# Keys and values of a cross attention, made in the prologue or inside the units that use them later

## The reference, cut to what matters

```python
q = xn @ Wq                       # xn: x normalised twice, (2, 512, 128)
kv = context @ Wkv                # (2, 154, 96) @ (96, 2048)
k, v = jnp.split(kv, 2, axis=-1)
dots = jnp.einsum('bhnd,bhmd->bhnm', q, k) * scale
dots = jnp.where(mask, dots, -jnp.inf)
attn = jax.nn.softmax(dots, axis=-1)
out = jnp.einsum('bhnm,bhmd->bhnd', attn, v)
return out.reshape(...) @ Wo + bo
```

## Time and profile before

| | us |
|---|---|
| median of 3 runs (lowest, highest) | 501.18 (499.8, 506.23) |
| span of the profiled execution | 502.9 |
| prologue up to the first scores | 33.0 |
| first scores to the transposes of unit 0 | 22.3 |
| one unit of the first cross attention | 12.4 |
| PE, DVE, ACT, POOL busy, whole span | 418.0, 315.5, 239.3, 72.2 |

### The profile page before, as it was taken

One profiled execution on the slowest core, in us unless ns is written; L12 is line 12 of the kernel. 1 busy time (PEld: TensorE's weight loads), 2 busy tenths in 40 slices (PEclk: granted clock), 3 DMA queues, 4 the chain that ended last, 5 costly groups with the idle time before them and its releaser, 6 DMA issues.

```text
span 502.9 us, 6017 instructions
## 1 busy us (share of the span) xinstructions
PE 418.0 (83%) x1990; PEld 216.3 (43%) x1990; DVE 315.5 (63%) x830; ACT 239.3 (48%) x683; POOL 72.2 (14%) x104
## 2 busy tenths in 40 slices
PE   4978789899897999998575978578899997989576
PEld 2443445466453844676333644313222232324245
DVE  4555977666873337546888683296687768671242
ACT  2325566745663273302534654005577776577220
POOL 5260500001000010002397020300000002000110
PEclk9979999999999997999988898956999999999956
DMA  8900000000000000000000002703800000000000
GB/s 230 220 1 1 1 0 2 1 1 0 3 1 0 1 0 0 1 1 1 1 0 1 1 0 93 159 0 117 136 1 2 2 1 3 1 1 1 23 0 21
DMA packets 15742, 12.93 MB, mean 26 GB/s; under 512 B 2880, under 2 KB 14879, under 8 KB 15519
## 3 DMA queue, kind: packets, MB, share of 16 engines
q1 hardware_dynamic: 15150, 11.64, 9.8%
q10 hardware_dynamic: 561, 0.90, 0.7%
HBM read 8.80 MB, written 3.67 MB: 25 GB/s over the span
## 4 chain that ended last, share of the span: by engine, by line
PE 49%; DVE 27%; ACT 14%; DMA 5%; issue 3%; SPq 1%; ACTq 0%; POOL 0%; DVEq 0%
PE pC L637 6%; PE pT L686 6%; PE pS L536 5%; DVE PT L1067 5%; ACT PT L806 5%; PE pS L380 4%; PE pC L426 4%; PE pT L478 3%; PE pS L629 3%; DVE mx L1243 3%; DVE mx L1042 3%; DVE spare L1067 3%; PE pC L413 2%; PE pT L349 2%; ACT PT L920 2%
## 5 line engine op out<-in xcount | busy, mean ns | idle before, releaser
L1243 DVE TENSOR_REDUCE mx<-pS 128x2 f32<-128x1024 f32 x64 | 77.0, 1221 | 26.9 <-PE pS L629 26.8
L920 ACT ACTIVATE PT<-pT 128x512 f32<-128x512 f32 x128 | 72.8, 597 | 25.7 <-PE pT L686 23.5
L380 PE MATMUL pS<-space,xT 128*128 128x308 f32 x192 | 69.3, 471 | 8.3 <-ACT PT L806 2.9
L806 ACT ACTIVATE PT<-pS,nm 128x154 f32<-128x154 f32 x136 | 51.3, 400 | 47.1 <-DVE nm L1045 47.1
L1343 POOL TENSOR_SCALAR ve<-mv 128x4 f32<-128x4 f32 x10 | 2.3, 229 | 358.1 <-DVE mv L969 358.1
L686 PE MATMUL pT<-space 128*128 128x512 bf16 x128 | 47.7, 387 | 7.0 <-ACT PT L920 3.1
L629 PE MATMUL pS<-space 128*128 128x512 bf16 x128 | 43.3, 425 | 10.8 <-DMA space<-parts_scratch 4.9
L413 PE MATMUL pC<-PT,space 128*128 128x512 f32 (+2 forms) x144 | 49.4, 620 | 2.8 <-DVE PT L1054 1.5
L380 PEld LDWEIGHTS pS<-space,xT 128*128 128x128 f32 x192 | 35.2, 210 | 30.6 <-issue 16.6
L1042 DVE TENSOR_REDUCE mx<-pS 128x4 f32<-128x616 f32 x48 | 38.3, 797 | 11.5 <-PE pS L384 7.5
L1067 DVE TENSOR_SCALAR PT<-PT,rz 128x154 f32<-128x154 f32 x136 | 37.7, 341 | 1.2
(11 more groups left out here) (209 smaller groups left out, 662.1 us busy)
## 6 DMA issues: line engine op xcount, KB each, us to landing
space<-parts_scratch SPq DMA_DIRECT2D x8, 384.0 KB, 7.2
parts_scratch<-space SPq DMA_DIRECT2D x6, 256.0 KB, 2.4
parts_scratch<-space SPq DMA_DIRECT2D x2, 384.0 KB, 2.5
parts_scratch<-space SPq DMA_DIRECT2D x6, 128.0 KB, 2.3
space<-in_L_xattn_Wq_dram SPq DMA_DIRECT2D x1, 512.0 KB, 3.8
x<-in_x_dram SPq DMA_DIRECT2D x2, 256.0 KB, 6.8
space<-in_L_xattn_Wo_dram SPq DMA_DIRECT2D x1, 512.0 KB, 7.0
space<-in_L_ffn_up_w_dram SPq DMA_DIRECT2D x1, 512.0 KB, 6.0
```

What stands on the lines that cost most here:

```text
L380: last = mm(ps[:, 512 * i:512 * i + 2 * T], xT[:, b, q * P:(q + 1) * P], a.KP[:, b, G4 * g + 2 * i:G4 * g + 2 * i + 2, :].rearrange("p h k ...
L806: last = A.activation(pq(n, u, q)[:, j * T:(j + 1) * T], ps[:, c:c + T], ACT.Exp, bias=nm[:, u % 2, q, j:j + 1], scale=XSCALE, accum_out=z ...
L920: A.activation(PT[:, 4 * kt + j, :], ps[:, :], ACT.Exp, scale=SSCALE)\
L1243: V.tensor_reduce(mx[:, u % 2, k // 2, j:j + 2], ps[:, :].rearrange("p (i k) -> p i k", i=2), AX.X, ALU.max).then_inc(freed(("ss", u, k)), 1)
```

## The change

The prologue makes only the first four transposes of Wq and the keys of group 0 (two key blocks, four heads). Group 1's keys are made in the head of `cross` between scores 1 and 2 of unit 0; the second four transposes and group 2's keys in unit 0, group 3's in unit 1, after `turn(u)` and ahead of scores 2; batch 0's values stay in the head, batch 1's move into units 2 and 3 at the same place. KT holds eight heads instead of sixteen and moves into OT's space; the memsets of its zeros halve. On DVE the statistics of batch 0 stand ahead of the keys' copies, `normalise(0, 0)` and batch 1's statistics behind the mask's conversion, and the four instructions for `allow` move into the head of `cross`, behind group 1's copies. The second layer's calls have new arguments and the same content.

```diff
+        KH = 2 * G4
-            kt = m.take(H * B * T) if n else PT[:, 0:10, :].rearrange("p c s -> p (c s)")[:, 0:H * B * T]
-            a.KT = kt.rearrange("p (h b k) -> p h b k", h=H, b=B)
+            kt = m.take(KH * B * T) if n else OT_[:, 4 * S:4 * S + KH * B * T]
+            a.KT = kt.rearrange("p (h b k) -> p h b k", h=KH, b=B)
...
+            def group_keys(a, g):            # PE
+                keysT(a, (2 * g, 2 * g + 1))
+                for h in range(G4 * g, G4 * g + G4):
+                    keys(a, h)
...
                 scores(a, 0, 1)
                 if n == 0:
-                    context_values(a, 0, (0, 1, 2, 3, 4))
+                    group_keys(a, 1)
                 scores(a, 0, 2)
                 if n == 0:
-                    context_values(a, 1, (0, 1))
+                    context_values(a, 0, (0, 1, 2))
                 scores(a, 0, 3)
                 if n == 0:
-                    context_values(a, 1, (2, 3, 4))
+                    context_values(a, 0, (3, 4))
...
                     turn(u)
+                    if n == 0 and u == 0:
+                        weightsT(a, (4,))
+                        group_keys(a, 2)
+                    if n == 0 and u == 1:
+                        group_keys(a, 3)
+                    if n == 0 and u == 2:
+                        context_values(a, 1, (0, 1, 2))
+                    if n == 0 and u == 3:
+                        context_values(a, 1, (3, 4))
                     scores(a, u + 1, 2)
...
             context()
-            weightsT(xa[0])
-            keysT(xa[0])
-            for h in range(H0):
-                keys(xa[0], h)
+            weightsT(xa[0], (0,))
+            group_keys(xa[0], 0)
             columns()
...
-                exponentials(0, 0, 2)        # ACT, head of cross
+                exponentials(0, 0, 1)
+                if n == 0:
+                    group_keys(a, 1)
+                exponentials(0, 1, 3)
                 if n == 0:
                     act.wait_ge(consts, 1)
-                    context_values(a, 0, (0, 2, 4))
-                exponentials(0, 2, 3)
-                if n == 0:
-                    context_values(a, 1, (0,))
+                    context_values(a, 0, (0, 2))
                 exponentials(0, 3, 4)
                 if n == 0:
-                    context_values(a, 1, (2, 4))
+                    context_values(a, 0, (4,))
...
                     copy_chunk(u, 4)
                     copy_chunk(u, 2)
+                    if n == 0 and u in (0, 1):
+                        group_keys(a, u + 2)
+                    if n == 0 and u == 2:
+                        context_values(a, 1, (0, 2))
+                    if n == 0 and u == 3:
+                        context_values(a, 1, (4,))
...
                     maxima(a, 0, 0, 2)       # DVE, head of cross
-                    dve.wait_ge(consts, 1)
-                    context_values(a, 0, (1, 3))
+                    group_keys(a, 1)
+                    allowed()
                     maxima(a, 0, 2, 3)
                     divide(0, 0)
-                    context_values(a, 1, (1,))
+                    dve.wait_ge(consts, 1)
+                    context_values(a, 0, (1,))
                     maxima(a, 0, 3, 4)
                     divide(0, 1)
-                    context_values(a, 1, (3,))
+                    context_values(a, 0, (3,))
...
                     divide(u + 1, 1)
+                    if n == 0 and u == 0:
+                        weightsT(a, (4,))
+                    if n == 0 and u in (0, 1):
+                        group_keys(a, u + 2)
+                    if n == 0 and u in (2, 3):
+                        context_values(a, 1, (2 * u - 3,))
...
-            V.memset(xa[0].KT[DH:P, 0:H0:2, :, :], 0.0)
-            V.memset(xa[0].KT[0:DH, 1:H0:2, :, :], 0.0).then_inc(kt_pads, 1)
-            weightsT(xa[0])
-            keysT(xa[0])
-            for h in range(1, H0, 2):
-                keys(xa[0], h)
-                if h in (1, 5):
-                    statistics(0, h // 4)
-                if h == 11:
-                    normalise(0, 0)
+            V.memset(xa[0].KT[DH:P, 0:KH:2, :, :], 0.0)
+            V.memset(xa[0].KT[0:DH, 1:KH:2, :, :], 0.0).then_inc(kt_pads, 1)
+            weightsT(xa[0], (0,))
+            statistics(0, 0)
+            group_keys(xa[0], 0)
             dve.wait_ge(W["mask"], 16)
             V.tensor_scalar(maskb[:, :, :], masku[:, :, :], -BLOCKED, BLOCKED, ALU.mult, ALU.add)\
                 .then_inc(mask_ready, 1)
-            seq(V.tensor_copy(maskf[:, :, :], masku[:, :, :]))
-            (three more on allow; all four are now allowed())
+            normalise(0, 0)
+            statistics(0, 1)
             cross(xa[0])
```

More of the change, by code:

```diff
@@ L321, in columns, with weightsT @@
                 tr(ps[:, 0:E], gwr[:, :], ident[0:E, 0:E]).then_inc(full("gateT"), 1)
-            def weightsT(a):
+            def weightsT(a, firsts):
                 n = a.n
                 pe.wait_ge(W[f"Wq{n}"], 16)
-                for c0 in range(0, a.H // 2, 4):
+                for c0 in firsts:
                     ps = claim("T", ("wqT", n, c0))
@@ L336, in keysT @@
                 pe.wait_ge(ctx_pads, n + 1)
-                for c in range(a.H // 2):
+                for c in cs:
                     ps = claim("C", ("kT", n, c))
@@ L454, in cross @@
                 if n == 0:
-                    weightsT(xa[1])
-                    keysT(xa[1])
+                    weightsT(xa[1], (0,))
+                    keysT(xa[1], range(H1 // 2))
                     for h in range(4):
@@ L741, in xt, with keysT @@
                     cp(xT[:, b, :], ps[:, :]).then_inc(freed(("xT", stage, b)), 1)
-            def keysT(a):
-                for c in range(0, a.H // 2, 2):
+            def keysT(a, cs):
+                for c in cs:
                     ps = filled(act, ("kT", a.n, c))
@@ L747, in keysT @@
                         r = slice(DH * i, DH * (i + 1))
-                        last = cp(a.KT[r, 2 * c + i, :, :].rearrange("p b k -> p (b k)"), ps[r, 0:B * T])
+                        last = cp(a.KT[r, (2 * c + i) % KH, :, :].rearrange("p b k -> p (b k)"), ps[r, 0:B * T])
                     last.then_inc(freed(("kT", a.n, c)), 1)
@@ L765, in context_values, with group_keys @@
                     last.then_inc(freed(("v", n, b, k)), 1)
+            def group_keys(a, g):
+                keysT(a, (2 * g,))
+                for h in (G4 * g, G4 * g + 2):
+                    keys(a, h)
             def self_in(b):
@@ L833, in cross @@
                 if n == 0:
-                    keysT(xa[1])
+                    keysT(xa[1], range(0, H1 // 2, 2))
                     for h in (0, 2):
@@ L990, in weightsT, with keysT @@
                         .then_inc(freed(("wqT", a.n, c0)), 1)
-            def keysT(a):
-                for c in range(1, a.H // 2, 2):
+            def keysT(a, cs):
+                for c in cs:
                     ps = filled(dve, ("kT", a.n, c))
@@ L1013, in context_values, with group_keys @@
                     ins.then_inc(freed(("v", a.n, b, k)), 1)
+            def group_keys(a, g):
+                keysT(a, (2 * g + 1,))
+                for h in (G4 * g + 1, G4 * g + 3):
+                    keys(a, h)
             def parts(u):
@@ L1117, in cross @@
                 if n == 0:
-                    weightsT(xa[1])
-                    keysT(xa[1])
+                    weightsT(xa[1], (0,))
+                    keysT(xa[1], range(1, H1 // 2, 2))
                     for h in (1, 3):
```

18 lines of the change are left out of this document (9 added, 9 removed).

## The result

The changed kernel takes 516.66 us (median of four runs, 513.29 to 518.41) against 503.71 us for the kernel before, timed beside it: a ratio of 1.029 with a 95% interval of 1.024 to 1.034. It is slower, and by more than the 8.8 us of the forecast.

What follows compares the result with a forecast made beforehand. PE's own queue was taken as the chain within a unit, nearly full in both places. Units' 18.05 us less 10.4 us gained earlier gave +7.7, 508.9 us by the median; +1.0 for the clock made 510 us, range 504 to 517.

Steps and rivals of the forecast that it cites:

- The start: Prologue: with less work there, the first scores issue at 19.7 us, 13.3 us earlier.
- The head: First scores to unit 0's transposes: these start at 43.9 us, keeping 11.3 of 13.3 us; gain up to scores 2, 10.4 us.
- the sum: Unit costs of 18.05 us less 10.4 us gained earlier: +7.7 us, 508.9 us by the median.
- The units: Units 0 to 3: extra work ahead of scores 2 costs 5.7, 5.7, 3.75 and 2.9 us, together 18.05.
- the clock's term: Head of the attention: PE's new wait may bring the clock down, costing 2.0 us; half taken, +1.0 us.
- The verdict's side: Whole kernel: within 2% (10.0 us) counts as same, chance 0.58; slower 0.38, faster 0.04.
- The range: Whole kernel: 504 to 517 us, leaving out the not-slower case and a little above the 514.5 us rival.
- The page's rule: Trainium skill page: frequent short idles between matmul groups, from cycling through PSUM, let the clock swing; would make 514.5 us likely.
- The rival of falls in the ping-pong of units 0 and 1: Units 0 and 1: clock falls during key making, two of up to 1.8 us, give 514.5 us; chance 0.22.
- The rival on the other side: Units 0 to 3: copies' round trips overlap PE's gaps, units cost 6.15 us, total 496.9 us; chance 0.14.

Runs made afterwards that it cites:

- the spread kernel: Changed kernel with only the place of the extra work inside units 0 to 3 altered, set between scores and values: 503.94 us, ratio 1.007 to the kernel before.
- The second profile of before: Profile of the unchanged kernel before, timed again against itself with no edit: 501.02 us, ratio 0.999.
- all three profiles of the changed kernel: Profiles of three measurements of the same changed kernel, without edits: 516.66, 512.39 and 512.55 us, ratios 1.029, 1.023 and 1.021 to the kernel before.
- the filled one: Changed kernel with unread transposes in four of PE's waits and unit 0's chunk 4 ahead of chunk 3: 509.01 us, ratio 1.012 to the kernel before.
- the mended kernel with the chunk order: Changed kernel with work spread in units, head reordered, normalise(0, 1) after unit 0's work, unit 0's chunk 4 ahead of chunk 3: 500.09 us, ratio 0.998.
- filled: The mended kernel with the chunk order, plus 21 unread transposes in three of PE's waits: 496.74 us, ratio 0.988 to the kernel before.
- the later measurements: The same changed kernel timed a second and a third time, no edit: 512.39 and 512.55 us, ratios 1.023 and 1.021 to the kernel before.
- the kernel with the head mended: Changed kernel with mask row-sum instructions behind maxima 2 and value chunk 0 copied ahead of tile 2's exponentials: 509.24 us, ratio 1.018 to the kernel before.
- the late normalisation: Changed kernel with work spread and head reordered, plus DVE's normalise(0, 1) moved to the end of unit 0's work: 499.89 us, ratio 0.996 to the kernel before.

## Why the prediction came out as it did

**The start** was right: 19.7 us forecast, 19.72 measured, and by the forecast's own path (last key copy, mask, normalisation, transposes, xT). It was right by terms that cancel: the last key copy ended at 16.71 us, 1.4 later than taken, while the mask's conversion, no longer beside POOL's memsets, took 0.47 us instead of 1.25, and xh's transposes 0.63 us instead of the 1.12 of the earlier trace rows, which ran at half clock.

**The head** was right in its places (PE behind value chunk 0's copy, then DVE's divides), at 44.37 against 43.9. Its end was short: 8.7 us of gain were left at the weights' transposes of unit 0 (50.82 us, against scores 2 at 59.48 before) where the sum had 10.4. Of the 1.9 us by which that point came later than the forecast 48.95, 0.5 stand in the start of the transposes; the wait ahead of their second part, 3.33 us, was some 0.7 longer than the sum had it, and a fall of the clock stretched the second part from 0.93 to 1.59 us.

**The units** were right: 6.0, 5.9, 3.8 and 2.9 us against 5.7, 5.7, 3.75 and 2.9 by the first profile, and the spread kernel shows that the part called round trips could be had back. In the stretch between the insertions of units 0 and 1 another 1.1 us came back: scores 2 of unit 1 stand 2.17 us behind those of before, those of unit 0 2.65 us ahead, a step of 4.8 where the insertion alone is 5.9. Most of it is PE's wait ahead of the second part of unit 1's transposes, 1.54 us before and 0.65 us after; why it shrank isn't shown. POOL no longer ran there beside DVE; but it ran one unit later instead, and the wait that came behind it there was 0.65 us too. Sum: 18.6 - 8.7 - 1.1 = 8.8 us up to the landmark, where the two profiles show 8.9 and the forecast for them was 7.7 + 1.0.

**The step that failed is the clock's term.** It was written as +1.0 us, half the price of one fall in the head. Two things were wrong in it. First, the profile that the sum started from had itself a fall, 6.7 us at half clock from 31 us, and the sum carried it over into the new kernel's start as if it belonged to the program. The second profile of before has none and is 2.4 us faster at the landmark. The sum also set the profile's span of 502.9 beside a median of times; a span is 1.7 us shorter than the time of its execution (511.6 and 513.29), so that execution of before was 3.4 us above the median of 501.18 and not 1.7. The sum itself, median plus 7.7, is not touched by that, but the sign that the profile was of a long execution was overlooked. Second, a fall in unit 0 was priced at nothing in the forecast and stood only among the rivals, with 0.22, as one in the ping-pong; all three profiles of the changed kernel have it, the filled one too.

The first and the third profile of the changed kernel are 11.7 us at half clock up to 60 us on average, the two of before 3.4. The price can be taken from pairs of profiles of one kernel, counted from the start of the xh transposes to the landmark so that the landing of the first transfers stays out: before, 135.08 us with 6.7 us at half clock and 132.51 with none; after, 156.74 with 13.3 and 155.25 with 10.1; the mended kernel with the chunk order, 146.23 with 6.8, and filled, 143.91 with none. That is 0.38, 0.47 and 0.34 us for a microsecond at half clock, each from a single pair. The 8.3 us of difference are then some 3 to 4 us, an estimate, where the sum had 1. Over whole executions the record's mean clocks agree with the size of the difference: 11 to 13 us more at half clock in the later measurements than in before.

Between the first two profiles an estimate from the clock agrees with the account by steps: 7.7, less the 1.1 that came back, plus 2 to 3 for 6.7 us more at half clock, against 8.9 at the landmark. The tails are nearly alike (336.6 and 336.8 us against 336.8 and 335.6). That the first measurement shows 13.0 and not 8.7 us has to do with which executions were profiled: that of after was the fastest of its four (513.29 against a median of 516.66), that of before lay 0.9 us above the median of 503.71. And those four executions of after were 86 us at half clock on average, where the later ones were 73; at 0.2 to 0.4 us each that is 3 to 5 us, about the 4 by which they were slower. That is an estimate from a correlation; where in the kernel these falls lay, no profile shows.

**The verdict's side** followed from that. 510 us was inside two per cent of 501.18 with 0.58; with a clock term of 3 to 4 it would have been 512 to 513, and slower the likelier. The range, 504 to 517, held 516.66 only just, and by the first measurement's surplus, which the sum doesn't explain.

**The page's rule.** The rival of falls in the ping-pong of units 0 and 1 (514.5 us) came out in part. The page "TensorE: Matmul & The Clock Gate" of the Trainium skill, section "A second HAM failure mode: psum-queue depth-cycling", has TensorE's short idles between groups of matmuls, made by cycling through PSUM, let the clock swing; the traces agree with it only in part. Against both: unit 1 has the same ping-pong as unit 0, and from 60 to 160 us the granted clock is 1.00 in all three profiles of the changed kernel; the falls in the head and in unit 0 began behind single longer waits (2.7 and 3.3 us), ahead of the ping-pong. For them: in the six profiles with this ping-pong the fall in unit 0 lasted 10.2 us twice, 6.8 us once and 3.4 us three times; in the five with the extra work spread it lasted 3.4 us three times and didn't come twice. And in the kernel with the head mended a fall began at 68.7 us, inside unit 1's ping-pong:

```profile
68.21 4.00 PE L350 MATMUL pT<-OT,space 128*128 128x308 f32 x8 [0.45 <-issue]
```

These products took 4.00 us where unit 1's in the first profile took 2.70. Part of what the spread kernels gained may be this; they were not built to tell. Why the fall at the start comes in some executions and not in others of one program is not settled here.

**The rival on the other side** (waits filled, not slower) was wrong for this kernel and became right when the order made it so: with the extra work spread and the head mended the time is that of the kernel before, and 0.4% better with the late normalisation.

## What to carry to other kernels

Moving work out of a prologue buys nothing when the engine that does it is as full in the new place; what counts is whether its round trips land beside other work of that engine's queue, so put a dependent chain's steps between independent ones, not in a block. A new order also opens new waits of TensorE: look for each one of some microseconds, price the fall of its clock behind it, and count it as a chance, not as a certainty. Before a sum is made from one profile, look whether its own granted clock had a fall in the stretches that the change touches.

## What was not expected of the hardware

Work without a use made a kernel faster: 21 transposes into waits took the ratio from 0.998 to 0.988, with the granted clock at 1.00 up to 60 us. It did not always do so: in the changed kernel 12 of them ahead of a longer wait left 1.59 us of it, and the fall came. The same program with the same wait of 1.52 us had a fall of the clock in one execution and none in another. The mask's conversion on DVE took 1.25 us beside POOL's memsets and 0.47 us without them; its cast from uint8 1.47 us and 0.47 us, both of the same shape. POOL's memsets in the first profile of before (the conversion stands at 29.69, the cast at 30.86), and the cast of the kernel after, beside which POOL does nothing:

```profile
29.48 1.12 POOL L1380 MEMSET space<- 64x1232 f32 x1
30.66 1.34 POOL L1381 MEMSET space<- 64x1232 f32 x1
...
30.21 0.47 DVE L1076 CAST OT<-PT 128x616 f32<-128x616 uint8 x1
```
